# Graph layer on one core: window-end sums alone are stored, the gather ring goes from 40 to 66 slots, queries pass through DRAM

## What is computed

```python
xn = _layernorm(x)
x = x + _L0_gnn_ref(xn, stack([src, dst]), ...) + _L0_mix_ref(xn[None], ...)[0]
x = x + _L0_ffn_ref(_layernorm(x)[None], ...)[0]
```

## Time and profile before

| | us |
|---|---|
| median of 3 runs (lowest, highest) | 1491.21 (1490.78, 1492.29) |
| the profiled execution, its span | 1489.6 |
| TensorE busy | 1175.3 (79%) |
| VectorE busy | 996.3 (67%) |
| GpSimd busy | 692.2 (46%) |
| ScalarE busy | 499.2 (34%) |

### The profile page before, as it was taken

One profiled execution on the slowest core, in us unless ns is written; L12 is line 12 of the kernel. 1 busy time (PEld: TensorE's weight loads), 2 busy tenths in 40 slices (PEclk: granted clock), 3 DMA queues, 4 the chain that ended last, 5 costly groups with the idle time before them and its releaser, 6 DMA issues. The chain is left out here.

```text
span 1489.6 us, 30544 instructions
## 1 busy us (share of the span) xinstructions
PE 1175.3 (79%) x6192; PEld 946.9 (64%) x6193; DVE 996.3 (67%) x2854; ACT 499.2 (34%) x1969; POOL 692.2 (46%) x782
## 2 busy tenths in 40 slices
PE   4996699999999878666672799999991799999900
PEld 4664466666666656444451688888881689999800
DVE  6565388888888867665674588899965234444378
ACT  2453233333333322221121655555521123333301
POOL 1001765666666566666621457676753011111175
PEclk9898599999999998787795799999995799999955
DMA  6062678888888777676757534334413972222155
GB/s 194 30 109 78 142 238 247 238 240 249 249 253 246 234 221 224 207 213 197 222 149 218 195 125 135 127 134 139 143 53 129 343 257 70 70 70 70 61 166 179
DMA packets 219212, 255.70 MB, mean 172 GB/s; under 512 B 57205, under 2 KB 193016, under 8 KB 215640
## 3 DMA queue, kind: packets, MB, share of 16 engines
q1 hardware_dynamic: 177464, 140.79, 30.0%
q0 software_dynamic: 30992, 103.79, 24.1%
q10 hardware_dynamic: 10640, 9.86, 2.1%
HBM read 139.69 MB, written 114.67 MB: 171 GB/s over the span
## 5 line engine op out<-in xcount | busy, mean ns | idle before, releaser
L738 POOL DMA_INDIRECT rows<-node_rows,srcT x391 | 389.0, 995 | 217.5 <-PE pO L1048 107.6
L1048 PE MATMUL pO<-rows,pw 128*128 x1184 | 337.2, 416 | 33.5 <-DVE pw L819 29.4
L835 DVE SCALAR_TENSOR_TENSOR acc<-acc,rsc,pO 128x257 f32<-128x257 f32 x592 | 281.0, 475 | 60.2 <-PE pO L1048 29.9
L1048 PEld LDWEIGHTS pO<-rows,pw 128*128 128x128 f32 x1184 | 216.5, 202 | 78.7 <-issue 51.7
L1408 PE MATMUL pW_<-W_again,aT 128*128 128x256 f32 x800 | 183.1, 383 | 0.4 <-DVE res L1476 0.4
L1408 PEld LDWEIGHTS pW_<-W_again,aT 128*128 128x128 f32 x800 | 149.8, 192 | 19.5 <-DVE res L1476 0.7
L1854 POOL DMA_DIRECT2D ys_rows<-ye x64 | 34.5, 539 | 238.0 <-DVE ye L1805 238.0
L1744 ACT ACTIVATE hT<-pHe,b 128x128 f32<-128x128 f32 x256 | 73.0, 368 | 192.8 <-PE pHe L1770 174.8
L1770 PEld LDWEIGHTS pHe<-xeT,w1e 128*128 128x128 f32 x1024 | 127.4, 196 | 13.7 <-DVE w1e L1795 10.5
L1770 PE MATMUL pHe<-xeT,w1e 128*128 128x128 f32 x1024 | 128.1, 279 | 9.9 <-DVE xeT L1788 9.9
L1779 PE MATMUL pYe<-w,hT 128*128 x512 | 122.1, 382 | 1.2 <-issue 0.6
(11 more groups left out here) (332 smaller groups left out, 1929.1 us busy)
## 6 DMA issues: line engine op xcount, KB each, us to landing
agg_rows<-acc SPq DMA_DIRECT2D x296, 256.0 KB
w<-in_ffn_w SPq DMA_DIRECT2D x32, 512.0 KB, 5.8
xe<-xs_rows ACTq DMA_DIRECT2D x64, 128.0 KB, 2.0
ys_rows<-ye POOLq DMA_DIRECT2D x64, 128.0 KB, 2.0
rows<-node_rows,srcT POOLq DMA_INDIRECT x391
node_rows<-xna SPq DMA_DIRECT2D x25, 136.0 KB, 1.8
xna<-in_x SPq DMA_DIRECT2D x5, 640.0 KB, 11.2
mix_rows<-hx SPq DMA_DIRECT2D x25, 128.0 KB
```

The costliest lines, as they stand in the source:

```text
L738: pool.indirect_dma_start(rows[:, k % RING, :], None, node_rows[:, :], at_row(srcT[:, k:k + 1])).then_inc(s_rows[k % len(s_rows)], 16)
L835: dve.scalar_tensor_tensor(out=acc[:, k % V3, s % HG, 0:D + 1], in0=before, scalar=rsc[:, g % V2, s:s + 1], in1=pO[n % PB][:, 0:D + 1], op ...
L1048: pe.matmul(pO[n % PB][:, 0:D + 1], pw[:, s // HG, s % HG, :], rows[:, ds(at[s % 4], 1), 0:D + 1].rearrange("p c f -> p (c f)"), start=Tru ...
```

## The change

- **Stores.** Only the last sum of each window is stored: 196 DMAs of 128 KB to `agg_win`, from the highest window down. SP runs them as one list: for a window it loads from a table (`win_tab`) the step at which it ends and the place of that sum in `acc`, waits until VectorE has done so many steps, and issues the store. Four stores are in flight at most (STORES).
- **Freeing acc.** As the stores of a half are no longer a fixed number, ScalarE runs `free_acc`: for each half it loads four numbers from `half_tab`, waits for the four store semaphores to reach them, and releases the half to VectorE.
- **The other DMAs of SP** (`load_flags`, `store_x2`, `store_top`, `load_tops`) move to ScalarE's queue.
- **Ring.** RING 40 becomes 66, LEAD 48 becomes 128, so `free_at` lets GpSimd fetch further ahead. The ring's memory now also holds, at other times, W and its transpose, `y`, `x2`, and buffers of the experts.
- **Queries.** `qT` is gone: each tile's queries are stored to `q_rows` by SP and loaded again in the edge stage by ScalarE (`load_q`, one a turn) into `qTb`.
- **Nodes out.** `AG` is loaded by a plain DMA of SP (`load_sums`), behind the loads of W and x2 in its list; GpSimd's `gather` and `last_row` are gone.
- **Tables.** VectorE makes `win_tab` and `half_tab` (`window_slots`, `half_stores`) between the tiles of stage 1.

```diff
-RING, FLY, LEAD, AHEAD = 40, 4, 48, 2
+RING, FLY, LEAD, AHEAD = 66, 4, 128, 2
+STORES = 4
@@ stage 1
-            W = sb("W", [P, KD, H, D], ctx=ctx)
+            W = part(0, KD, H, D)
+                    def store_q(t, c, r):
+                        wait(sp, qT_sb, t)
...
+                        sp.dma_start(out_q, qTo[:, c, :, :].rearrange("p k f -> p (k f)")).then_inc(s_q[c], 16)
+                    def window_slots():
...
+                    def half_stores():
...
@@ edges, VectorE
-                                dve.wait_ge(s_agg[k % V3], turns_of(k))
+                                wait(dve, acc_free, k - V3)
@@ edges, ScalarE
-                    groups([(1, mean_square), (1, copy_h), (1, fifth), (1, last_flags), (1, last_max), (3, keep_den(0)), (3, keep_den(1)), (1, shrink), (1, exps), (0, copy_eq),
-                            (1, copy_top), (0, copy_on), (0, copy_as)])
+                    def free_acc(i):
+                        def stage(g):
+                            k = 2 * g + i
+                            if k < 2 * GROUPS - V3:
+                                stored = [act.value_load(half_tab[0:1, k, c:c + 1], min_val=1, max_val=16 * WINDOWS + 1) for c in range(STORES)]
+                                for c in range(STORES):
+                                    act.wait_ge(s_agg[c], stored[c])
+                                act.sem_inc(acc_free.sem, 1)
+                        return stage
+
+                    def load_q(t):
+                        if t < NT:
+                            wait(act, num_ps, t - 2)
+                            act.dma_start(qTb[:, t % 2, :, :].rearrange("p k f -> p (k f)"), q_rows[t, :, :]).then_inc(s_q[t % 2], 16)
+
+                    def load_next_q(g):
+                        load_q(g + 1)
+                    load_q(0)
+                    groups([(2, load_tops), (0, load_next_q), (1, mean_square), (1, copy_h), (1, store_x2), (1, fifth), (0, load_flags), (1, last_flags), (1, last_max), (3, keep_den(0)), (3, free_acc(0)), (3, keep_den(1)), (1, shrink), (1, exps), (0, copy_eq),
+                            (1, copy_top), (1, store_top), (0, copy_on), (3, free_acc(1)), (0, copy_as)])
@@ edges, SP
-                    def store(i):
-                        def stage(g):
-                            k = 2 * g + i
-                            for q in range(PARTS):
-                                wait(sp, acced, g, i * HG + (q + 1) * HP)
-                                sp.dma_start(agg_rows[k * HG + q * HP:k * HG + (q + 1) * HP, :, :].rearrange("s p f -> p s f"),
-                                             acc[:, k % V3, q * HP:(q + 1) * HP, 0:D]).then_inc(s_agg[k % V3], 16)
-                        return stage
+                    for w in range(WINDOWS):
+                        r, c, turn = WINDOWS - 1 - w, w % STORES, w // STORES
+                        steps = sp.value_load(win_tab[0:1, r, 0:1], min_val=1, max_val=GROUPS * G)
+                        place = sp.value_load(win_tab[0:1, r, 1:2], min_val=0, max_val=ACCS - 1)
+                        sp.wait_ge(acced.sem, steps)
+                        if turn:
+                            sp.wait_ge(s_agg[c], 16 * turn + 1)
+                        sp.dma_start(agg_win[r, :, :], acc_slot[:, ds(place, 1), 0:D].rearrange("p c f -> p (c f)")).then_inc(s_agg[c], 16)
@@ nodes out
+                    def load_sums(t, c, r):
+                        wait(sp, agg_in, t - 2)
...
+                            sp.dma_start(AG[:, c, :, :].rearrange("p h f -> p (h f)"), row(by_node, t)).then_inc(s_AG[c], 16)
-                    pipeline(sp, NT, [(0, load_x), (7, store)])
+                    pipeline(sp, NT, [(0, load_sums), (0, load_x), (7, store)], extra=3)
-                    pipeline(pool, NT, [(0, gather), (2, with_x), (3, with_bias), (6, with_beta), (8, scatter)])
+                    pipeline(pool, NT, [(2, with_x), (3, with_bias), (6, with_beta), (8, scatter)])
```

More of the change, by code:

```diff
@@ L405, in _ @@
                     for j in range(2):
-                        mm = pe.matmul(pE[:, 448:448 + NT], same_win, by_tile[:, j, :], start=(j == 0), stop=(j == 1))
+                        pe.matmul(ended_ps, ones[:, 0:1], ended[:, j, :], start=(j == 0), stop=(j == 1))
+                    for j in range(2):
+                        mm = pe.matmul(ends_of[:, j * P:(j + 1) * P], cnt[:, j:j + 1], ident, start=True, stop=True)
                     mm.then_inc(steps_ps, 1)
@@ L633, in build @@
             moves.expect(2)
-            V2, V3, PB = 2, 3, 4
-            rows = sb("rows", [P, RING, RW], ctx=ctx)
+            qTb = sb("qTb", [P, 2, KD, P], ctx=ctx)
+            q_stored = [16 * len(range(c, NT, 2)) for c in range(2)]
             asb = sb("asb", [P, V2, G, H], ctx=ctx)
@@ new lines, in store_x2, with store_top @@
+                    @node_tile
+                    def store_x2(t):
+                        wait(act, mixed, t)
+                        act.dma_start(row(mix_rows, t), hx[:, t % 2, :]).then_inc(s_x2[t % 2], 16)
+                    def store_top(g):
+                        wait(act, td_in, g)
+                        by_half = top_rows.rearrange("(t s) w -> t (s w)", s=HG)[2 * g:2 * g + 2, 0:P * MW]
+                        act.dma_start(by_half.rearrange("i (p c) -> p i c", c=MW), topd[:, g % V2, :, :]).then_inc(s_top, 16)
@@ L1114, in _ @@
                     sp.dma_start(mbo[:, :], a["mix_b_out"].partition_broadcast(1)).then_inc(consts.sem, 16)
-                    @node_tile
-                    def store_x2(t):
-                        wait(sp, mixed, t)
-                        sp.dma_start(row(mix_rows, t), hx[:, t % 2, :]).then_inc(s_x2[t % 2], 16)
                     sp.wait_ge(s_gad, 16 * SJ)
@@ L1150, in _ @@
-                    groups([(0, load_flags), (2, load_tops), (1, store_x2), (2, store(0)), (1, store_top), (2, store(1))])
+                    for c in range(STORES):
+                        sp.sem_inc(s_agg[c], 1)
+                    for w in range(WINDOWS):
[6 more added lines that the diff above has]
+                        sp.dma_start(agg_win[r, :, :], acc_slot[:, ds(place, 1), 0:D].rearrange("p c f -> p (c f)")).then_inc(s_agg[c], 16)
@@ L1639, in build @@
         b1 = sb("b1", [P, E, FK], ctx=experts_ctx)
-        b2 = sb("b2", [P, E, D], ctx=experts_ctx)
+        b2 = part(Y_END, E, D)
         WS = 2
```

190 lines of the change are left out of this document (111 added, 79 removed).

## The result

The changed kernel took 1596.8 us (median of 4 runs, 1588.3 to 1601.1) against 1491.7 us for the kernel before: ratio 1.070, 95% interval 1.067 to 1.073. (A fourth run of the kernel before took 2627 us; the ratio leaves it out.) The change costs 105 us; the forecast was 70, with a range from 1466 to 1606 us.

What follows compares the result with a forecast made beforehand. The prediction took a loop through ScalarE's tail, without slack ahead of TensorE's scores, to set the early beat. Its terms, 1 + 65 - 6 + 10 = +70 on a span of 1489.6, gave 1561 us as median, range 1466 to 1606.

Steps and rivals of the forecast that it cites:

- Slower, and by ScalarE's tail: Edge stage: ScalarE's additions between last transpose and asb delay each group by about 3 us; chance 0.50.
- The price of the additions: ScalarE's tail: four loads at 0.60 us, waits 0.2 and an issue 0.34 make asb 2.9 us later (2.3 to 3.9).
- the first faster rival: ScalarE's tail: loads overlap each other, so the additions don't delay the scores; 1469 us, chance 0.15.
- The early groups: First 21 beats of the edge stage: each 3.1 us longer (2.5 to 4.1), +65 us (51 to 86).
- a rival, 1593 us: Early groups: TensorE's clock falls after idle time ahead of the scores, 1.5 us more a group; 1593 us, chance 0.13.
- The two issues behind asb: ScalarE behind asb: load_q and store_x2 ahead of zlow add 0.3 us a group.
- ScalarE's tail has no slack: Early beat: TensorE loads the weights of scores 0.1 us after asb, so ScalarE's tail was read as without slack.
- The late groups: Last 13 beats: the ring removes the wait for rows, register loads put nearly that back; -6 us (-31 to +3).
- Ahead of the edge stage: First stage: query stores, small VectorE operations and matmuls mostly hidden by TensorE's work; +1 us (0 to 3).
- The stage of the nodes: Node stage: AG's plain loads stand behind those of x and land 13 us late, part comes back; +10 us (0 to 14).
- SP: SP's window loop: about 2.2 us a window, just under a beat; as slower rival at 2.6 us, 1586 us, chance 0.06.

Runs made afterwards that it cites:

- e3: Changed kernel with the four register loads of free_acc(1) done twice: 1785.2 us, ratio 1.135 to the kernel before on its chip.
- e6: Changed kernel with the four loads of free_acc(1) only moved, from ahead of asb to ahead of copy_top: 1639.7 us, ratio 1.042 to the kernel before.
- e2: Changed kernel with store_top issued behind asb, load_q and store_x2 behind zlow: 1693.6 us, ratio 1.075 to the kernel before.
- e9: Kernel before with only the two register loads of copy_as moved ahead of copy_top: 1578.3 us, ratio 1.002 to the kernel before.
- e8: Changed kernel with e7's edits, one free_acc load and copy_as's loads ahead of copy_top, DMA issues moved later: 1629.6 us, ratio 1.036 to the kernel before.
- e12: e8 with RING 40, LEAD 48, flag stores back on SP and three query buffers for two: 1585.5 us, ratio 1.013 to the kernel before.
- e7: Changed kernel with flag_rows stores on GpSimd's queue and the first two AG loads ahead of x2's: 1696.8 us, ratio 1.079 to the kernel before.
- e5: Changed kernel without any edit, run again on another chip: 1703.9 us, ratio 1.081 to the kernel before there.
- e11: e8 with LEAD back at 48 and the 66 slots kept: 1615.2 us, ratio 1.027 to the kernel before.

## Why the prediction was right, and where it was off

**Slower, and by ScalarE's tail: right.** The direction, the place and most of the size came from the loop. The traces of the first chip have 3.1 of the 4.3 us a group between topd and asb. e3 and e6 show with the same instructions, doubled and moved, that the place is what costs: +81 and -64 us.

**The price of the additions: right.** The step said that asb comes 2.9 us later (2.3 to 3.9); it came 3.2 us later (5.23 less 2.04). A load with its check was put at 0.60 us; they stand 0.53 to 0.66 apart, 0.28 the load alone. The issue was put at 0.34, what ScalarE needs to issue; it moved the copy behind it by 0.52, and e2, which takes it out of the tail, gets that back. The loads run one after the other, so the first faster rival (they overlap) had nothing to it. By the Trainium skill, "DMA: Bandwidth & Descriptors", section "Latency and other measured facts", a tensor_load takes about 600 ns at least; the median of 284 here is 279 ns, so the measurement decides.

**The early groups: mis-sized.** Forecast 3.1 us a group, +65; measured 4.3, +89.5. Of this the tail is 3.2 by 21, 67 us. The other 22 us, 1.1 a group, I put down to TensorE's clock: behind its 2.8 us of idle time it did scores and products at the slower of the two rates of the earlier trace rows, and from the start of the scores to that of L1097 the quoted turn takes 3.81 us (403.62 to 407.43), against 2.33 in the quiet turn of e9 (221.76 to 224.09). The table of the loop has the rest of the loss just there, 1.30 us between the scores and the matmul that reads zT, and a granted clock of 0.93 instead of 1.00 over 19.25 us is 1.3 us of work at full speed (an estimate from the stage table). That fits, but no run changed the clock by itself, so the cause of these 22 us is argued and not shown. I had priced just this at 1.5 us a group as a rival, 1593 us, and given it 0.13. That the measured 1596.8 lies beside it is partly luck: the clock took 22 us and not 31, and 10 are of the query buffers. The two rows it rested on, 0.46 us after 2.11 and 0.77 after 4.15 of idle time, stand on either side of 2.8, and the forecast took the good one without a reason. It should have had an even chance.

**The two issues behind asb: wrong.** The sum had +0.3 us a group for `load_q` and `store_x2` ahead of zlow, 6 of the 65. The traces have nothing of it: ScalarE is idle ahead of zlow for 0.5 us a group, before as after (means of groups 6 to 22): zlow waits for TensorE's L1091, and from the start of the scores to zlow are 1.4 us instead of 0.9, so that TensorE's slower matmuls hide the two issues. Seen with the row above, the sum had 0.3 in the wrong place and nothing for the matmuls.

**"ScalarE's tail has no slack": half right.** TensorE loaded the weights 0.1 us after asb, and I read that as the cause. It was a tie: four products kept TensorE busy up to the same moment, and it was busy ahead of the scores in every early group. For the forecast it made next to no difference, since with either reading an addition is paid but for some 0.1 us. It made two wrong expectations behind it, e9 and e8, where I took time out of the tail. The two readings differ only for a removal. That the forecast came through this is luck: nothing in it had looked at what else TensorE did up to then.

**The late groups: right in kind.** Forecast -6, measured +0.2. The wait for rows is gone (but for the first group, `fetched` was never waited for), and the tail has its place: before, the 13 late tails were some 42 us over 2.04 each in sum; now they are 13 by 3.0, 39 us. Which part of the change ended the wait, the ring, the lighter stores or the later asb, stays open: it was seen on the first chip alone, and no run there took one of them back.

**Ahead of the edge stage: wrong.** I put +1 (0 to 3) on it, since TensorE's work hides the additions; it was +11.1. The step looked at what the store adds to engines and not at the two buffers behind it. In the changed kernel a query store issued beside a flag store landed after 6.1 and 6.8 us, the others after 1.7 to 1.8: 4 to 5 us late, more than the one tile of 3.5 us that two buffers allow, and ScalarE stands; the third buffer of e12 took most of it back, and e7 shows that the wait doesn't need the flag stores on SP's queue.

**The stage of the nodes: right.** +10 for +11.1 to the first `own`. Of it 7.9 us is the loads of AG behind those of x2, which e7 gives back, and 3.2 the longer way from the last `spread` to the last `acc`.

**SP: right to leave out of the sum.** Its windows hardly ever held an accumulator: 0.7 us in all at the waits of `free_acc`.

So the span grew by 40 us more than forecast: 22 in the early groups beyond the tail (the clock, as argued), 10 by the query buffers, 6 in the late groups and 5 in small terms, less the 3.5 us gained behind the first `own`.

## What to carry to other kernels

Before you add register loads, waits or DMA issues to an engine that is a third busy, look at where in its program they stand: in a wait that is long enough they were free here (e6, e9), between the instruction that ends the wait and the one another engine waits for they were paid every round (e3), and moving them costs nothing. Two instructions that end within 0.1 us of each other don't tell which of them is the bound: the price of an addition can be read from it, the gain of a removal only by checking what else the waiting engine does in that time. With a double buffer in front of a store, count the longest time to land among everything else on the DMA engines, not the usual one. And when a comparison is repeated on another chip, compare it stage by stage: the same ratio can be another sum.

## What the runs showed of the hardware

The chips of the experiments were slower for the same program in two places, in the stage of the groups and at the end: behind the last product of the experts the rest took 91 us (e5, e9) instead of 77 to 78. Both have gathers of GpSimd. In the stage of the groups the instructions of several engines came late at the same time. The stores of SP from 190 us on, first the changed kernel on the first chip to 319 us, then on the chip of e5 (min/median/max ns of the issue):

```profile
L1220 SPq DMA_DIRECT2D agg_win<-acc x54: 338/339/377, 194.7 to 319.2; - x54
```

```profile
L1220 SPq DMA_DIRECT2D agg_win<-acc x34: 4/339/728, 195.7 to 319.6; - x34
```

The issues of 4 and of 728 ns come in bursts, with starts some 0.70 to 0.73 us apart or right behind each other, on SP, ScalarE and GpSimd together, also for register operations that wait for nothing. In e8, ScalarE's address computations for asb, 55 ns each in a quiet group, did this:

```profile
L971 ACTq FUSED_REGOPS  x12: 5/18/722, 363.5 to 366.9; - x12
```

```profile
L971 ACTq FUSED_REGOPS  x9: 55/55/60, 380.0 to 381.0; - x9
```

In the two traces of the first chip no register operation took over 0.21 us. It reads like an instruction stream that is supplied late, but no run separates that from other causes, and the 38 packets of the instruction queue q8 (16 KB each) took hardly longer, a median of 1.10 us in e5 and 1.02 on the first chip; it stays open, as does why these chips and not the first. What the runs do show is that it was worst in the first five beats where gathers ran far ahead: with the release at 128 steps these took 135 to 144 us and held 21 to 32 register operations of over 0.65 us, with 48 steps (e9 too) 92 to 100 us and 4 to 11. The 18 beats behind them have 10 to 44 in every run on these chips, e9 included, but their number doesn't go with the length of these beats (10 and 18.2 us in e9, 44 and 18.5 in e11).
